# A gated delta-rule layer on one core: setup memsets split over three engines, the last batch's z moved into its scan, and the gating and storing of complete batches moved forward

## The chip, the cores and the metric

The kernel runs on one core of one Trainium2 chip. The metric is the device time of one execution in microseconds (us); lower is better. The other seven cores are idle. All arithmetic is fp32.

The engines are named as the profile names them: PE is TensorE (matmuls; PEld are its weight loads), DVE is VectorE, ACT is ScalarE, POOL is GpSimd, SP is SyncE, which issues most DMAs here. Each runs its own list of instructions in order, and they meet at semaphores only.

## The reference, cut to what matters

For four batches of 512 tokens of width 256:

```python
xn = layernorm(x)
s  = attn(xn)                    # below
g  = silu(ffn(xn))               # router, 8 experts, a shared expert
out = x + s * g

# attn: 32 value heads on 16 key heads, 128 wide
mixed = silu(causal_conv4(xn @ W_qkv));  q, k, v = split(mixed)
z = xn @ W_z
beta = sigmoid(xn @ W_b);  decay = -exp(A_log) * softplus(xn @ W_a + dt_bias)
for t in range(T):               # per batch and head, S is 128x128
    S = S * exp(decay[t])
    S = S + beta[t] * outer(k[t], v[t] - k[t] @ S)
    o[t] = q[t] @ S
s = (rmsnorm(o) * norm_w * silu(z)) @ W_out
```

## The kernel before, in words

Three blocks of code run one after the other. `prepare_block` normalises x and makes the decays. `ffn_block` computes `gate` = silu(ffn), 16 tiles of 128 tokens by 256, kept in SBUF. It ends at about 433 us. `recurrent_block` is the rest and the place of the change.

`recurrent_block` walks 16 key heads (i) by 4 batches (b), 64 steps, all unrolled. A step works on one batch and the two value heads of one key head, in four chunks of 128 tokens. It is a software pipeline over three batches: while step (i, b) projects and convolves q, k, v of batch b, it also scans the batch before it (b-1), and gates, transposes and projects out the one before that (b-2). The output of each head is summed into `acc` (128 x 16 tiles x 256) by `add_out` (L1209), one half batch at a time. The order on every engine is written out by hand; `counts(i, b)` (L598) turns a step into semaphore values, which all start from BASE.

*The setup* (L1030 to L1052, L1227 to L1245, L1437 to L1443, L787 to L790). Each engine raises its own semaphores, 7 on POOL, 14 on ACT, 16 on DVE and 21 on PE. DVE then clears eleven tiles, PSUM bank TRI and small rows; POOL clears z and acc; ACT clears nothing. All four wait until `init` is 5. SP meanwhile loads the first weights, cols and `sums_row` (1 MB, L609). Then POOL runs `log_decays` (L1420), which needs `sums_row`; ACT scales the output weights, and runs `exp_decay` (L1016) on POOL's result before its first `first_tap` (L1044).

*The scan* is four helpers on each engine. For chunk c, PE: `read_state` (L675, two products with the 128x256 state; the second into the OUT bank), `solve` (L685, the inverse times the residual, into the SCAN bank), `attend` (L700, the state's update at L706 and the scores' product at L713). ACT: `take_state_part` (L966), `take_updates` (L960, the copy `upd`), `squares` (L974). DVE: `residual` (L1161), `new_state` (L1170), `output` (L1183). One chunk's chain is read, residual, solve, upd, update, new state, and round again.

*After step 63* the last scan (batch 3 of the last head) has no step to hide in. PE runs `join_w` to `gated_transpose`, then all four pieces of `project_z` for batch 3, two to a PSUM bank (Z_BANK, banks 5 and 3), waiting for ACT's `gate_z` (L995) between the halves and once more before the output projection, whose OUT_BANK is bank 3 as well. Then four chunks of scan with one piece of `project_out` (batch 2) in each. Then POOL's `output_norms` (L1406), DVE's `gating` (L1197), PE's transposes (L948) and `project_out` for batch 3, and the two `add_out` halves. Then DVE multiplies all four batches of `acc` by `gate` (L1396), adds x to all four (L1401, from `x_back`, tiles whose work is over, loaded by SP from L662), raising `final` for each, and SP, which waits for `final` to be 4, stores four batches of 512 KB (L664 to L667) and waits for them.

Of the kernel before, what the change touches and what calls it, by code (L numbers as in the profile page):

```python
# [14 lines left out]
ALU = mybir.AluOpType  # L15
# [457 lines left out]
def recurrent_block(nc, x, w_in_dram, w_z_dram, w_out_dram, norm_dram, keep, g_rows, out):  # L473
# [10 lines left out]
    with ExitStack() as ctx:  # L484
# [72 lines left out]
        GT_BANK, OUT_BANK, Z_BANK = (0, 2), (3, 1), (5, 3)  # L557
# [29 lines left out]
        x_in, stored, final = sem("x_in"), sem("stored"), sem("final")  # L587

        XT = NL + 1
        X8 = 2 * R - 2  # L590
# [12 lines left out]
        def _(sp):  # L603
# [60 lines left out]
            sp.wait_ge(final, BATCH)  # L664
            for b in range(BATCH):
                sp.dma_start(out[b].rearrange("(c p) d -> p c d", p=P), acc[:, b * NC_:(b + 1) * NC_, :]).then_inc(stored, 16)
            sp.wait_ge(stored, 16 * BATCH)  # L667
# [3 lines left out]
        def _(pe):  # L671
# [68 lines left out]
            def project_z(tb, c):  # L740
                for m in range(KT):
                    last = nc.tensor.matmul(ps[Z_BANK[c // 2]][:, (c % 2) * D:(c % 2 + 1) * D],  # L742
                                            xnT[:, m, tb * T + c * C:tb * T + (c + 1) * C], w_z[:, m, :],
                                            start=(m == 0), stop=(m == KT - 1))
                if c % 2:
                    last.then_inc(z_ps, 1)
# [43 lines left out]
            pe.wait_ge(init, 5)  # L790
# [140 lines left out]
            for c in range(NC_):  # L931
                project_z(BATCH - 1, c)
                if c == 1:
                    pe.wait_ge(z_done, n(2) + 1)
            for c in range(NC_):
                if c:
                    read_state(c)
                solve(c)
                if c == 0:
                    pe.wait_ge(z_done, n(2) + 2)  # L940
                project_out(n, c, NK + 1)
                attend(c)
# [12 lines left out]
        def _(act):  # L955
# [39 lines left out]
            def gate_z(n, h):  # L995
# [3 lines left out]
                nc.scalar.activation(z[:, 2 * h:2 * h + 2, :], ps[Z_BANK[h]][:, :].rearrange("p (c d) -> p c d", c=2),  # L999
# [30 lines left out]
            for s in (decay_done, conv0_done, mixed_done, ksq_done, qsq_done, v_done, wq_done, w32_done, w64_done,  # L1030
                      z_done, fs_done, upd_done, osq_done, gT_done):
                act.sem_inc(s, BASE)
            act.wait_ge(norm_in, 16)
            act.wait_ge(init, 5)
# [106 lines left out]
            gate_z(n, 0)  # L1141
            gate_z(n, 1)
            for c in range(NC_):
                if c:
                    take_state_part(c)
                take_updates(c)
                squares(c)
# [5 lines left out]
        def _(dve):  # L1153
# [77 lines left out]
            for t in (qkT[1], v[1], kw[1], scores[1], inv[0], inv[1], invT, bmat, xq, xqT, o):  # L1231
# [13 lines left out]
            dve.wait_ge(init, 5)  # L1245
# [132 lines left out]
            halves(n, 1)  # L1378
            for c in range(NC_):
# [4 lines left out]
                output(c)  # L1384
            add_out(n, BATCH - 2, 0)
            add_out(n, BATCH - 2, 1)
            n = counts(NK, 1)
            for g in range(REP):
                gating(n, g)
            add_out(n, BATCH - 1, 0)  # L1390
            add_out(n, BATCH - 1, 1)

            dve.wait_ge(acc_done, n(2) + 2)
            for b in range(BATCH):
                at = slice(b * NC_, (b + 1) * NC_)
                nc.vector.tensor_tensor(acc[:, at, :], acc[:, at, :], gate[:, at, :], ALU.mult).then_inc(acc_done, 1)  # L1396
            dve.wait_ge(x_in, 16 * BATCH)
            dve.wait_ge(acc_done, n(2) + 2 + BATCH)
            for b in range(BATCH):
                row = acc[:, b * NC_:(b + 1) * NC_, :].rearrange("p c d -> p (c d)")  # L1400
                nc.vector.tensor_tensor(row, row, x_back[b], ALU.add).then_inc(final, 1)  # L1401
# [3 lines left out]
        def _(pool):  # L1405
# [33 lines left out]
            for t in (z, acc):  # L1439
                nc.gpsimd.memset(t[:, :, :], 0.0).then_inc(init, 1)  # L1440
            pool.sem_inc(init, 1)
            pool.wait_ge(init, 5)
# [167 lines left out]
```

## Time and profile before

| | |
|---|---|
| runs (us) | 2793.66, 2805.60, 2795.55; median 2795.55 |
| profiled execution, its own time | 2802.01 |
| its span, first to last instruction | 2800.1 |
| mean granted TensorE clock | 0.985 of 2.4 GHz |
| busy: PE, DVE, ACT, POOL | 94%, 71%, 58%, 38% |
| prepare and FFN blocks end, recurrence's setup begins | about 433 |
| first matmul of step 0 | 445.88 |
| first matmul after step 63 (the last `join_w`) | 2736.29 |
| last output of the scan done | 2767.93 |
| first store issued | 2792.07 |

How to read it: rows of a timeline give the start in us from the span's beginning, the length, the engine and line, output <- input, and how many instructions were merged; in square brackets how long the engine had idled before it and who released it. A length of merged rows is from the first's start to the last's end. A PE group's busy end is modelled, so the start of the next group tells more than the length. SPq is SP's queue issuing a DMA. PEclk is the granted clock: 1.00 is 2.4 GHz, 0.50 is 1.2 GHz.

### The profile page before, as it was taken

The page shows a single profiled execution, that of the slowest core. Times are in us where ns is not written, and L with a number is a line of the kernel's source. Part 1 is how long each engine was busy: PE and PEld are TensorE (multiplying, and loading weights), DVE is VectorE, ACT ScalarE, POOL GpSimd, SP SyncE. Part 2 cuts the span into 40 slices and gives each one's busy share as a digit, 9 for nine tenths or more (in the row PEclk, how much of TensorE's full clock was granted, in tenths as well). Part 3 has the DMA queues.
Part 4 walks back from the last instruction along what each step waited for, and adds up shares of the span by engine and source line. Part 5 has one row for each costly group of instructions (what it writes and reads, how often), then busy time and mean ns, then how long its engine had stood idle before and what let it go on. Part 6 is the DMA issues. An engine that isn't in the chain of part 4 may idle for free.

```text
span 2800.1 us, 87430 instructions
## 1 busy us (share of the span) xinstructions
PE 2619.4 (94%) x34330; PEld 1946.0 (69%) x34330; DVE 2001.6 (71%) x4880; ACT 1610.8 (58%) x5046; POOL 1075.5 (38%) x1391
## 2 busy tenths in 40 slices
PE   2999997999999999999999999999999999999995
PEld 2456655777777777777777777777777777777774
DVE  5322235888878887888778877887778878888773
ACT  2111114666666666666666666666666666666662
POOL 0312203444444444444444444444444444444440
PEclk8999998999999999999999999999999999999997
DMA  4322301111111111111111111111111111111112
GB/s 148 76 53 64 64 1 53 46 54 46 53 46 54 46 54 46 54 46 54 46 53 46 54 46 53 47 43 49 43 49 50 49 49 50 50 50 50 50 50 64
DMA packets 225654, 146.99 MB, mean 52 GB/s; under 512 B 187456, under 2 KB 195936, under 8 KB 225120
## 3 DMA queue, kind: packets, MB, share of 16 engines
q1 hardware_dynamic: 219104, 123.58, 15.5%
q0 software_dynamic: 6144, 17.83, 2.8%
q8 instruction: 275, 4.51, 0.7%
q14 instruction: 131, 1.07, 0.1%
HBM read 115.81 MB, written 2.70 MB: 42 GB/s over the span
## 4 chain that ended last, share of the span: by engine, by line
PE 66%; DVE 8%; ACT 3%; issue 2%; DMA 2%; SPq 1%; POOL 1%; DVEq 0%; POOLq 0%; ACTq 0%
PE rps L809 12%; PE rps L734 8%; PE rps L742 8%; DVE conv L1262 6%; PE rps L696 4%; PE rps L826 4%; PE rps L713 4%; PE rps L865 3%; PE rps L856 3%; PE rps L839 3%; PE rps L680 3%; PE rps L706 3%; PE rps L774 3%; PE rps L783 3%; PE rps L683 2%
## 5 line engine op out<-in xcount | busy, mean ns | idle before, releaser
L1262 DVE SCALAR_TENSOR_TENSOR conv<-rps,w_in,conv 128x509 f32<-128x509 f32 (+2 forms) x768 | 572.0, 745 | 64.6 <-ACT conv L1050 46.4
L809 PE MATMUL rps<-xnT,w_in 128*128 128x512 f32 x1024 | 504.3, 615 | 13.9 <-DVE cols L1244 13.0
L1461 POOL TENSOR_TENSOR decay_b<-decay,beta_k 128x512 f32<-128x512 f32 x128 | 130.6, 1042 | 487.6 <-DVE beta_k L1278 487.6
L1412 POOL TENSOR_TENSOR o_t<-o_sq,q_mean 128x8 f32<-128x8 f32 x65 | 13.4, 206 | 691.0 <-ACT gated L983 691.0
L809 PEld LDWEIGHTS rps<-xnT,w_in 128*128 128x128 f32 x1024 | 174.8, 190 | 148.2 <-issue 125.2
L742 PE MATMUL rps<-w_z,xnT 128*128 128x256 f32 x1040 | 275.1, 387 | 1.0 <-ACT z L999 0.7
L1050 ACT ACTIVATE conv<-rps,w_in 128x512 f32<-128x512 f32 x256 | 176.1, 688 | 164.5 <-PE rps L809 161.5
L734 PE MATMUL rps<-w_outn,gatedT 128*128 128x256 f32 x1056 | 241.3, 381 | 1.0 <-ACT gatedT L993 0.7
L734 PEld LDWEIGHTS rps<-w_outn,gatedT 128*128 128x128 f32 x1056 | 201.6, 191 | 49.7 <-issue 23.8
L1064 ACT ACTIVATE qkT<-conv 128x512 f32<-128x512 f32 x128 | 80.5, 629 | 222.1 <-DVE conv L1262 222.1
L742 PEld LDWEIGHTS rps<-w_z,xnT 128*128 128x128 f32 x1040 | 183.1, 191 | 21.6 <-ACT z L999 1.1
L964 ACT ACTIVATE upd<-rps 128x256 f32<-128x256 f32 x260 | 100.0, 385 | 158.9 <-PE rps L696 158.3
L983 ACT ACTIVATE gated<-o 128x128 f32<-128x128 f32 x520 | 155.1, 304 | 59.7 <-DVE o L1188 57.4
L435 DVE TENSOR_TENSOR silu_g<-fps_u,silu_g 128x512 f32<-128x512 f32 x51 | 35.3, 692 | 196.6 <-PE fps_u L458 196.6
L1022 ACT ACTIVATE decay<-log_d,cols 128x128 f32<-128x128 f32 x520 | 165.9, 395 | 5.0 <-POOL log_d L1435 4.3
L1435 POOL TENSOR_TENSOR log_d<-log_d,sums_row 128x512 f32<-128x512 f32 x130 | 163.3, 1277 | 5.4
L398 POOL DMA_DIRECT2D scale<-comb_rows x96 | 64.2, 679 | 247.6 <-DVE hid L424 187.2
L713 PE MATMUL rps<-upd,scores 128*128 128x128 f32 x1040 | 158.4, 275 | 0.0
L1337 DVE TENSOR_TENSOR xq<-rps,xq 128x256 f32<-128x256 f32 x128 | 53.9, 421 | 142.1 <-PE rps L865 142.1
L1206 DVE SCALAR_TENSOR_TENSOR gated<-o,o_r,z 128x128 f32<-128x128 f32 x528 | 151.4, 344 | 2.2 <-POOL o_r L1418 2.1
L1167 DVE SCALAR_TENSOR_TENSOR resid<-rps,cols,v 128x128 f32<-128x128 f32 x390 | 118.3, 345 | 43.9 <-PE rps L680 43.7
L409 ACT ACTIVATE silu_g<-fps_g 128x512 f32<-128x512 f32 x68 | 40.6, 597 | 189.0 <-PE fps_g L458 189.0
(217 smaller groups left out, 6477.4 us busy)
## 6 DMA issues: line engine op xcount, KB each, us to landing
sums_row<-g_rows SPq DMA_DIRECT2D x65, 1024.0 KB, 5.0
scale<-comb_rows POOLq DMA_DIRECT2D x40, 256.0 KB, 5.0
w_in<-in_w_in SPq DMA_DIRECT2D x17, 520.0 KB, 3.5
bq<-bmat SPq DMA_DIRECT2D x256, 32.0 KB, 2.0
inv<-xq SPq DMA_DIRECT2D x256, 32.0 KB, 1.9
w_z<-in_w_z SPq DMA_DIRECT2D x17, 256.0 KB, 2.6
w_out<-in_w_out SPq DMA_DIRECT2D x17, 256.0 KB, 5.0
invT<-xqT SPq DMA_DIRECT2D x128, 32.0 KB, 2.2
```

Of the source, the lines that this page charges most:

```text
L713: last = nc.tensor.matmul(ps[OUT][:, g * P:(g + 1) * P], scores[r][:, g * NC_ + c, :], upd[:, g * P:(g + 1) * P], start=True, stop=True)
L734: last = nc.tensor.matmul(ps[OUT_BANK[c // 2]][:, (c % 2) * D:(c % 2 + 1) * D], gatedT[:, g, c * C:(c + 1) * C], w_outn[:, g, :], start=(g ...
L742: last = nc.tensor.matmul(ps[Z_BANK[c // 2]][:, (c % 2) * D:(c % 2 + 1) * D], xnT[:, m, tb * T + c * C:tb * T + (c + 1) * C], w_z[:, m, :] ...
L809: last = nc.tensor.matmul(ps[PROJ_BANK[j]][:, :], w_in[:, m * 4 * P + j * P:m * 4 * P + (j + 1) * P], xnT[:, m, b * T:(b + 1) * T], start= ...
L983: last = nc.scalar.activation(gated[:, c, g * P:(g + 1) * P], o[:, c, g * P:(g + 1) * P], ACT.Square, accum_out=o_sq[:, u:u + 1])
L1022: last = nc.scalar.activation(decay[:, u, :], log_d[:, u, :], ACT.Exp, bias=col(k, NLO, u))
L1050: nc.scalar.activation(conv[:, j, :], ps[PROJ_BANK[j]][:, :], ACT.Copy, scale=w_in[:, KT * 4 * P + j * KC + KC - 1:KT * 4 * P + (j + 1) * ...
L1167: nc.vector.scalar_tensor_tensor(resid[:, g * P:(g + 1) * P], ps[SCAN][:, g * P:(g + 1) * P], col(k, NGAM, u), v[r][:, u, :], ALU.mult, AL ...
L1206: nc.vector.scalar_tensor_tensor(gated[:, c, part], o[:, c, part], o_r[:, u:u + 1], z[:, c, part], ALU.mult, ALU.mult).then_inc(gated_done, 1)
L1262: nc.vector.scalar_tensor_tensor(conv[:, j, shift:T], ps[PROJ_BANK[j]][:, 0:T - shift], w_in[:, k:k + 1], conv[:, j, shift:T], ALU.mult, A ...
L1435: nc.gpsimd.tensor_tensor(log_d[:, us, :], log_d[:, us, :], sums_row[:, 1, us, :], ALU.add).then_inc(g_done, 1)
L1461: nc.gpsimd.tensor_tensor(decay_b[:, us, :], decay[:, us, :], beta_k2[:, us].unsqueeze(2).to_broadcast([P, NC_, C]), ALU.mult).then_inc(db ...
```

## The change

Four edits, all in `recurrent_block`.

1. Setup: DVE keeps qkT, v, kw, bmat, xq, xqT and the small ones; POOL clears inv[0], inv[1], invT and z; ACT clears scores[1], o and acc, by a copy of a constant column with scale 0. `init` counts 9.
2. z of batch 3: the block of four `project_z` calls ahead of the last scan goes. Each chunk now has one between `solve` and `project_out`. The second half goes to bank 4 instead of 3, and PE's two waits for `z_done` go. ACT's two `gate_z` calls move from before the scan to behind `take_updates` of chunks 1 and 3.
3. Gate and x: batch 0's product with `gate` stands behind `output(0)` of the last scan, batch 1's behind `output(1)`, batch 0's x behind `output(2)`, batch 1's x behind the two `add_out` of batch 2. Batch 2 has both behind the last `gating`. Batch 3 is done in halves of 128x512, each as add, product, x.
4. Stores: SP stores batches 0 to 2 each as `final` reaches 1, 2, 3, and batch 3 in two halves of 256 KB at 4 and 5.

```diff
-        GT_BANK, OUT_BANK, Z_BANK = (0, 2), (3, 1), (5, 3)
+        GT_BANK, OUT_BANK, Z_BANK, LAST_Z = (0, 2), (3, 1), (5, 3), (5, 4)
...
+        INIT = 9
...
-            sp.wait_ge(final, BATCH)
-            for b in range(BATCH):
+            for b in range(BATCH - 1):
+                sp.wait_ge(final, b + 1)
                 sp.dma_start(out[b].rearrange("(c p) d -> p c d", p=P), acc[:, b * NC_:(b + 1) * NC_, :]).then_inc(stored, 16)
-            sp.wait_ge(stored, 16 * BATCH)
+            for h in range(2):
+                sp.wait_ge(final, BATCH + h)
+                sp.dma_start(out[BATCH - 1].rearrange("(c p) d -> p c d", p=P)[:, 2 * h:2 * h + 2, :],
+                             acc[:, TILES - NC_ + 2 * h:TILES - NC_ + 2 * h + 2, :]).then_inc(stored, 16)
+            sp.wait_ge(stored, 16 * (BATCH + 1))
...
@@ tensor, after step 63
             for c in range(NC_):
-                project_z(BATCH - 1, c)
-                if c == 1:
-                    pe.wait_ge(z_done, n(2) + 1)
-            for c in range(NC_):
                 if c:
                     read_state(c)
                 solve(c)
-                if c == 0:
-                    pe.wait_ge(z_done, n(2) + 2)
+                project_z(BATCH - 1, c, LAST_Z)
                 project_out(n, c, NK + 1)
                 attend(c)
...
@@ scalar, setup
+            for t in (scores[1], o, acc):
+                flat = t[:, :, :].rearrange("p a n -> p (a n)")
+                nc.scalar.activation(flat, cst[:, IDENT:IDENT + 1].to_broadcast(list(flat.shape)), ACT.Copy, scale=0.0).then_inc(init, 1)
@@ scalar, after step 63
-            gate_z(n, 0)
-            gate_z(n, 1)
             for c in range(NC_):
                 if c:
                     take_state_part(c)
                 take_updates(c)
+                if c % 2:
+                    gate_z(n, c // 2, LAST_Z)
                 squares(c)
...
@@ vector, setup
-            for t in (qkT[1], v[1], kw[1], scores[1], inv[0], inv[1], invT, bmat, xq, xqT, o):
+            for t in (qkT[1], v[1], kw[1], bmat, xq, xqT):
                 nc.vector.memset(t[:, :, :], 0.0)
@@ vector, after step 63
+            def times_gate(tiles, done):
+                at = slice(*tiles)
+                dve.wait_ge(acc_done, done)
+                nc.vector.tensor_tensor(acc[:, at, :], acc[:, at, :], gate[:, at, :], ALU.mult).then_inc(mul_done, 1)
+
+            def plus_x(tiles, muls):
+                b, t0 = tiles[0] // NC_, tiles[0] % NC_
+                dve.wait_ge(x_in, 16 * BATCH)
+                dve.wait_ge(mul_done, muls)
+                row = acc[:, slice(*tiles), :].rearrange("p c d -> p (c d)")
+                nc.vector.tensor_tensor(row, row, x_back[b][:, t0 * D:(t0 + tiles[1] - tiles[0]) * D], ALU.add).then_inc(final, 1)
...
             for c in range(NC_):
                 if c:
                     residual(c)
                 if c < NC_ - 1:
                     new_state(c)
                 output(c)
+                if c < 2:
+                    times_gate(whole[c], n(2))
+                if c == 2:
+                    plus_x(whole[0], 1)
             add_out(n, BATCH - 2, 0)
             add_out(n, BATCH - 2, 1)
+            plus_x(whole[1], 2)
             n = counts(NK, 1)
             for g in range(REP):
                 gating(n, g)
-            add_out(n, BATCH - 1, 0)
-            add_out(n, BATCH - 1, 1)
-
-            dve.wait_ge(acc_done, n(2) + 2)
-            for b in range(BATCH):
-                at = slice(b * NC_, (b + 1) * NC_)
-                nc.vector.tensor_tensor(acc[:, at, :], acc[:, at, :], gate[:, at, :], ALU.mult).then_inc(acc_done, 1)
-            dve.wait_ge(x_in, 16 * BATCH)
-            dve.wait_ge(acc_done, n(2) + 2 + BATCH)
-            for b in range(BATCH):
-                row = acc[:, b * NC_:(b + 1) * NC_, :].rearrange("p c d -> p (c d)")
-                nc.vector.tensor_tensor(row, row, x_back[b], ALU.add).then_inc(final, 1)
+            times_gate(whole[BATCH - 2], n(2))
+            plus_x(whole[BATCH - 2], 3)
+            for h in range(2):
+                add_out(n, BATCH - 1, h)
+                times_gate(part[h], n(2) + h + 1)
+                plus_x(part[h], 4 + h)
...
@@ gpsimd, setup
-            for t in (z, acc):
+            for t in (inv[0], inv[1], invT, z):
                 nc.gpsimd.memset(t[:, :, :], 0.0).then_inc(init, 1)
-            pool.sem_inc(init, 1)
-            pool.wait_ge(init, 5)
+            pool.wait_ge(init, INIT)
```

`whole` lists the tiles of each batch, `part` the two halves of batch 3. The waits of PE, ACT and DVE for `init` change from 5 to `INIT` too.

## Rows read from the trace of the kernel before

**Rows 1.** The page's busy times of the engines (busy us, share of the span, instructions).
```profile
PE 2619.4 (94%) x34330; PEld 1946.0 (69%) x34330; DVE 2001.6 (71%) x4880; ACT 1610.8 (58%) x5046; POOL 1075.5 (38%) x1391
```
**Rows 2.** Timeline of the setup: start us, length us, engine line op, [idle before <-releaser].
```profile
435.04 3.51 POOL L1440 MEMSET acc<- 128x4096 f32 x1
435.36 0.91 DVE L1232 MEMSET qkT<- 128x1024 f32 x1 [32.19 <-issue]
...
435.98 0.59 SPq L609 DMA_DIRECT2D sums_row<-g_rows  x1
436.44 0.91 DVE L1232 MEMSET v<- 128x1024 f32 x1 [0.16 <-issue]
...
445.91 1.89 POOL L1426 TENSOR_TENSOR log_d<-sums_row,cols 128x1024 f32<-128x1024 f32 x1 [7.36 <-DVE cols L1244]
```
**Rows 3.** The view of line 609, the first sums_row load: issue to landing.
```profile
DMA to landing us min/median/max: 6.9/6.9/6.9
```
**Rows 4.** Timeline, ACT's decay exponentials of step 0.
```profile
451.86 2.45 ACT L1022 ACTIVATE decay<-log_d,cols 128x128 f32<-128x128 f32 x8 [3.93 <-POOL log_d L1435]
```
**Rows 5.** Timeline, PE from the z block to the first projection of the last scan.
```profile
2747.14 3.09 PE L742 MATMUL rps<-w_z,xnT 128*128 128x256 f32 x8
...
2752.81 0.61 PE L696 MATMUL rps<-v,inv 128*128 128x128 f32 x4
...
2753.72 1.13 PE L734 MATMUL rps<-w_outn,gatedT 128*128 128x256 f32 x4 [0.30 <-ACT z L999]
```
**Rows 6.** Timeline, the last scan's chunk 1 and the beginning of chunk 2.
```profile
2755.78 0.42 DVE L1193 COPY o<-rps 128x256 f32<-128x256 f32 x1
2755.81 0.70 PE L680 MATMUL rps<-state,qkT 128*128 128x256 f32 x2
...
2756.55 0.61 DVE L1167 SCALAR_TENSOR_TENSOR resid<-rps,cols,v 128x128 f32<-128x128 f32 x2 [0.34 <-PE rps L680]
...
2757.76 1.03 PE L734 MATMUL rps<-w_outn,gatedT 128*128 128x256 f32 x4
...
2758.62 0.61 PE L706 MATMUL rps<-upd,kw 128*128 128x128 f32 x4
...
2759.93 0.70 PE L680 MATMUL rps<-state,qkT 128*128 128x256 f32 x2 [0.25 <-DVE state L1177]
2760.67 0.61 DVE L1167 SCALAR_TENSOR_TENSOR resid<-rps,cols,v 128x128 f32<-128x128 f32 x2 [0.46 <-PE rps L680]
```
**Rows 7.** Timeline from the last scan's end to the stores.
```profile
2767.86 1.28 DVE L1212 TENSOR_TENSOR acc<-rps,acc 128x512 f32<-128x512 f32 x2
...
2769.31 1.64 POOL L1416 TENSOR_TENSOR o_n<-o_t,mhalf 128x8 f32<-128x8 f32 x1
...
2771.26 2.19 DVE L1206 SCALAR_TENSOR_TENSOR gated<-o,o_r,z 128x128 f32<-128x128 f32 x8 [2.13 <-POOL o_r L1418]
...
2780.10 0.69 DVE L1212 TENSOR_TENSOR acc<-rps,acc 128x512 f32<-128x512 f32 x1 [6.65 <-PE rps L734]
...
2782.67 4.63 DVE L1396 TENSOR_TENSOR acc<-acc,gate 128x1024 f32<-128x1024 f32 x4
...
2792.07 3.40 SPq L666 DMA_DIRECT2D out<-acc  x4
```
**Rows 8.** ACT's groups by shape: busy us, mean ns, idle before.
```profile
L964 ACT ACTIVATE upd<-rps 128x256 f32<-128x256 f32 x260 | 100.0, 385 | 158.9 <-PE rps L696 158.3
...
L993 ACT ACTIVATE gatedT<-rps 128x512 f32<-128x512 f32 x132 | 78.4, 594 | 22.7 <-PE rps L725 16.3 <-PE rps L948 6.4
```
**Rows 9.** Line 1206 from 445 to 451: duration in ns, min/median/max.
```profile
L1206 DVE SCALAR_TENSOR_TENSOR gated<-o,o_r,z x4: 342/1328/2089, 445.9 to 449.3; 128x128 f32<-128x128 f32 x4
```
**Rows 10.** Windows: busy us of PE, PEld, DVE, ACT, POOL; granted clock, DMA share, GB/s.
```profile
456.20:490.40 34.20, 33.26 (x438) 25.82 (x433) 26.02 (x66) 22.86 (x75) 13.99 (x16) 0.96 0.08 21
...
2749.50:2767.90 18.40, 15.56 (x84) 12.09 (x82) 4.94 (x16) 6.58 (x24) 0.00 (x0) 1.00 0.00 1
```
**Rows 11.** The view of line 666, the four stores: issue to landing.
```profile
DMA to landing us min/median/max: 3.0/4.6/5.5
```

More of the change, by code:

```diff
@@ L586, in recurrent_block @@
         b8_done, b8_ps, x8_done = sem("b8_done"), sem("b8_ps"), sem("x8_done")
-        x_in, stored, final = sem("x_in"), sem("stored"), sem("final")
+        x_in, stored, mul_done, final = sem("x_in"), sem("stored"), sem("mul_done"), sem("final")
         XT = NL + 1
+        INIT = 9
         X8 = 2 * R - 2
@@ L738, in project_out, with project_z @@
                     last.then_inc(out_ps, 1)
-            def project_z(tb, c):
+            def project_z(tb, c, banks=Z_BANK):
                 for m in range(KT):
-                    last = nc.tensor.matmul(ps[Z_BANK[c // 2]][:, (c % 2) * D:(c % 2 + 1) * D],
+                    last = nc.tensor.matmul(ps[banks[c // 2]][:, (c % 2) * D:(c % 2 + 1) * D],
                                             xnT[:, m, tb * T + c * C:tb * T + (c + 1) * C], w_z[:, m, :],
@@ L789, in _ @@
                 pe.sem_inc(s, BASE)
-            pe.wait_ge(init, 5)
+            pe.wait_ge(init, INIT)
             for i in range(NK):
@@ L993, in take_transposes, with gate_z @@
                 nc.scalar.activation(gatedT[:, g, :], ps[GT_BANK[g]][:, :], ACT.Copy).then_inc(gT_done, 1)
-            def gate_z(n, h):
+            def gate_z(n, h, banks=Z_BANK):
                 act.wait_ge(gated_done, n(8) + 8)
                 act.wait_ge(z_ps, n(2) + h + 1)
-                nc.scalar.activation(z[:, 2 * h:2 * h + 2, :], ps[Z_BANK[h]][:, :].rearrange("p (c d) -> p c d", c=2),
+                nc.scalar.activation(z[:, 2 * h:2 * h + 2, :], ps[banks[h]][:, :].rearrange("p (c d) -> p c d", c=2),
                                      ACT.Silu).then_inc(z_done, 1)
@@ L1032, in _ @@
                 act.sem_inc(s, BASE)
+            for t in (scores[1], o, acc):
+                flat = t[:, :, :].rearrange("p a n -> p (a n)")
+                nc.scalar.activation(flat, cst[:, IDENT:IDENT + 1].to_broadcast(list(flat.shape)), ACT.Copy, scale=0.0).then_inc(init, 1)
             act.wait_ge(norm_in, 16)
[L1034 removed]
+            act.wait_ge(init, INIT)
             scale_out_weights(1)
@@ L1244, in _ @@
             nc.vector.memset(cols[BATCH - 1][:, :], 0.0).then_inc(init, 1)
-            dve.wait_ge(init, 5)
+            dve.wait_ge(init, INIT)
             for i in range(NK):
@@ L1378, in _ @@
             halves(n, 1)
+            def times_gate(tiles, done):
[8 more added lines that the diff above has]
+                nc.vector.tensor_tensor(row, row, x_back[b][:, t0 * D:(t0 + tiles[1] - tiles[0]) * D], ALU.add).then_inc(final, 1)
+            whole = [(b * NC_, (b + 1) * NC_) for b in range(BATCH)]
+            part = [(TILES - NC_, TILES - 2), (TILES - 2, TILES)]
             for c in range(NC_):
```

## The prediction

> **What bounds the kernel now.** The page's busy shares come first: TensorE is busy 94% of the span [rows 1], nearly all of it in the 64 equal steps of the recurrence, which the diff does not touch. So only two stretches can change: the setup before step 0, and what follows step 63. I read the timeline of each, because a mean over the span hides both.
>
> Setup: DVE clears its tiles one after the other, a 1024-column tile each 1.08 us, from 435.36 on, while POOL is through with its largest one at 438.55. PE, ACT and POOL all start behind DVE's last memset, POOL's log decays at 445.91 [rows 2]. The sums_row load that these decays read was issued at 435.98 [rows 2] and took 6.9 us [rows 3], so it landed at 442.88. The first decay exponentials on ACT wait for POOL until 451.86 [rows 4], and ACT's first convolution copy stands behind them in its queue. So POOL's start places step 0.
>
> End: from 2747.14 PE does nothing but the last batch's z, before the scan's first solve at 2752.81 [rows 5]. Then come four scan chunks of 4.12 us each (read of the state at 2755.81, the next at 2759.93) [rows 6]; norms, gating, transposes and output projection until the first add at 2780.10; gate and x passes over all batches on DVE; and the stores, issued from 2792.07 [rows 7].
>
> **The change part by part.**
>
> *Memsets.* DVE loses four 1024-column tiles (scores, both inv, o) and the half-size invT. At 1.08 us a tile [rows 2] and about 0.6 for the half, 4.9 us: DVE would be done near 441.0, 4.9 before 445.9. POOL trades acc (4096 columns, 3.51 us [rows 2]) for 2560 more columns elsewhere and ends earlier than now. ACT gets 6144 columns in three activations. Its copies take 0.385 us for 256 columns and 0.594 for 512 [rows 8], 0.21 per 256 more: 1.0, 1.0 and 3.5 us. Starting near DVE's first memset, it ends near 441 too. Bounds for ACT: 5.5 us by that slope, 7.1 as twelve times the 512-column row; I take the slope, since one long instruction pays its start once, and even 7.1 ends at 442.5. That is below the next limit, sums_row at 442.88. POOL then starts near 442.95 instead of 445.91: **3.0 us**, where the memsets alone would give 4.9. PE's first projection starts earlier still, but its later work waits for ACT, behind POOL's decays.
>
> *The z block.* PE no longer runs z from 2747.14 to 2752.81 (5.67 us), nor waits 0.30 for ACT's z [rows 5]. Added are four pieces of z, one a chunk, between solve and projection. A piece has as many instructions of 256 columns as a projection piece, which takes 0.86 from its start to the next group's [rows 6] at the full clock; at the lower level it is half of 3.09, some 1.5 [rows 5]. What could hide it is the wait from solve to ACT's upd, but the projection fills that already: the group behind it starts 0.86 after it with no wait shown [rows 6]. So z costs its full price: 0.86 in each of chunks 1 to 3, and in chunk 0, partly at 1.2 GHz, 1.4, with 0.45 more because the first solve moves into that slow stretch. Chunk 1 begins 5.67 + 0.30 - 1.4 - 0.45 = 4.1 earlier; the three others give 2.6 back. ACT's two z activations (0.6 each [rows 8]) run while PE is in z and projection, and the next user, squares, waits for a later o: no cost.
>
> *Gate and x inside the scan.* A whole-batch pass takes 1.16 us, four in 4.63 [rows 7]. Three lie on DVE in chunks 0 to 2 (two gates, one x), between output(c) and residual(c+1). In the first gap DVE idles 0.34, in the second 0.46 [rows 6], so a pass delays the residual by 0.8, 0.7 and 0.7, and PE's solve stands right behind it: 2.2 lost. Bounds: 0 if DVE overlapped all of it, 3.5 if all three counted whole. The x pass of batch 1 stands behind the two add_outs, which end at 2769.14, and is done by 2770.3, before the gating's 2771.26 [rows 7]: hidden, 0.9 to spare. Both passes of batch 2 lie behind the gating, while PE transposes and projects until 2780.10: hidden, with several us of idle DVE left.
> Beside that x pass POOL works on the norms, 1.64 us of it in one instruction [rows 7]. Next to POOL's setup work DVE's gating, an instruction with two SBUF inputs, took up to 2.09 us where it otherwise takes 0.34 [rows 9]; the x pass has two SBUF inputs as well. The Trainium skill (GPSIMD Engine Reference, Key points) says that GpSimd shares its SBUF interfaces with VectorE and contends with such instructions. The row and this rule speak against that one place; POOL's operands there are 128x8 against 128x1024 in the setup, so the sum has no hold in it, and the hold is a rival.
> Scan in all: -4.1 + 2.6 + 2.2 = **0.7 us later**, if the clock stays full as now [rows 10].
>
> *The last batch.* From the first add (2780.10) to the first store issue (2792.07) are 11.97 us [rows 7]. New are six instructions of 512 columns (add, gate, x, twice). An add takes 0.69 [rows 7]; with about 0.05 for each wait on its own result, 4.4 us: **7.6 us** less. PE's second half is ready within the first three, so DVE sets this stretch.
>
> *Stores.* Now 8.0 us from the first issue to the end of the span. The fastest of the four 512 KB stores landed 3.0 us after its issue, the slowest 5.5 [rows 11]. Three now leave under other work, and the last one moves 256 KB. Bounds 2 and 3.5 us; I take 2.5 (the fastest, less what half the bytes save), and 0.5 to the last instruction: **5.0 us** less. SP waits in order, but each earlier final comes long before the next.
>
> Sum: 3.0 - 0.7 + 7.6 + 5.0 = **14.9 us**. The profiled execution took 2802.01 (span 2800.1), so it would take 2787.1. It lies 6.5 above the median of the runs, 2795.55, so the forecast is 2795.55 - 14.9 = **2780.6**. A measurement of this kernel can tell about 0.5%, 14 us, from no change: the sum is just beyond it.
>
> **The rivals.**
> *The memsets decide alone.* If sums_row landed earlier, the setup would give 4.9: 2778.7. Against it: the load's time hangs on the loads around it, and none of them moves.
> *A held DVE.* If POOL's 1.64 us norm holds the x pass as in [rows 9], the pass ends as late as 2772.2 and pushes the gating by up to 0.9: 2781.5. If the three passes in the scan also cost their whole 3.5 us, 2782.8. For: the same two engines did it in the setup. Against: the small operands.
> *The lower clock.* PE waits longer in each chunk. A chunk has about 3 us of PE work in its chain (z and projection 0.86 each; read, solve and update some 0.45 each, by groups of 0.6 to 0.7 that overlap [rows 6]). At 1.2 GHz that adds 3 us in three chunks and 2 in chunk 0: 11 us, 2791.6. Against: the scan idles already (15.56 us of work in 18.4) and is granted 1.00 [rows 10], and z adds work.
> *No earlier stores.* If the first three stores still left together with the last, 4 us of the five would be lost: 2784.6. The ascending counts on final speak against it.
> *Slower than before.* Step 0 begins after other gaps than now. It has 33.26 us of PE work in 34.2 at a mean clock of 0.96 [rows 10]. If PE, idle before its second projection, stayed at 1.2 GHz through the whole step, about 30 us would come on: 2810. Against: in the run shown it left that level early in the step. It decides against the change once half of the step is slow.
>
> **How the numbers follow.** Forecast 0.62, its own range 2777 to 2784; the terms' bounds and the spread of a median split it into 0.42 beyond 0.5% and 0.20 within. Memsets alone 0.08 (faster). Held DVE 0.16 (0.03 faster, 0.13 within). Lower clock 0.07 and late stores 0.05 (within). Slower 0.02. Together: faster 0.53, same 0.45, slower 0.02. The range goes from 2775 (memsets alone, a 2 us store, and a fast median) to 2788 (held passes, late stores and a slow median); the lower clock and the slower case stay out.
>
> **What would show it.** POOL's log decays 2.9 us earlier, behind the load and not behind a memset. Chunks of 5.6 to 5.8 us instead of 4.12, the residual late behind a DVE pass; the last output of the scan within 1 us of its old place. From the first add of the last batch to the last store issue 4.4 us, from there to the end 3. The forecast is wrong if PE's clock is 0.50 in the scan, if z costs a chunk nothing (2.6 us more won), if the load lands at another time, or if one of the 64 steps changes its length.

## The result, and the profile after

| us | before | after |
|---|---|---|
| median (lowest to highest) of nine runs each, on the same chip | 2800.76 (2793.66 to 2805.60) | 2787.56 (2786.54 to 2795.24) |
| profiled execution, own time (span) | 2802.01 (2800.1) | 2787.04 (2785.2) |

The ratio after to before is 0.9956, with a 95% interval from 0.9947 to 0.9965: 12.3 us faster, between 9.8 and 14.8, which is just inside the 0.5% that was called the bound. The two profiled executions differ by 14.9 us, the medians by 13.2.

The page after shows the same shares as before [rows 1], so it says nothing of where the time went:

```profile
PE 2622.0 (94%) x34330; PEld 1947.0 (70%) x34330; DVE 1994.5 (72%) x4877; ACT 1614.6 (58%) x5049; POOL 1073.6 (39%) x1393
```

The stages do. Each boundary of this table is the start of one row in the timelines; the times are differences between such starts, in us.

| stage | before | after | gain |
|---|---|---|---|
| FFN's last ACT instruction to POOL's first log decays | 12.97 | 10.00 | 2.97 |
| from there to the last `join_w` (64 steps) | 2290.38 | 2288.93 | 1.45 |
| last `join_w` to the last output's combination on DVE | 31.22 | 32.06 | -0.84 |
| from there to DVE's gating (norms) | 3.75 | 4.60 | -0.85 |
| gating to the last batch's first add | 8.84 | 8.69 | 0.15 |
| first add to the end of DVE's work | 11.94 | 4.33 | 7.61 |
| from there to the end of the span | 8.06 | 3.26 | 4.80 |

That is 15.3 us; the FFN ended 0.39 later, which leaves the 14.9. The diff has nothing in the 64 steps, so the 1.45 there isn't its doing: over the fourteen profiles of this study that stage lies between 2286.4 and 2297.6 us. That spread is as large as the one between the runs of one kernel, and probably the reason for it, though the profiles, which are of different kernels and chips, can't show that. The other stages repeat more closely: from the last `join_w` to the end, a second profile of this kernel and one with another order of loads took 52.5 and 53.5 us against 52.94 here.

**Setup.** The timeline of the kernel after, from the memsets to step 0's log decays:

```profile
434.95 1.06 ACT L1035 ACTIVATE scores<-cst 128x1024 f32<-128x1024 f32 x1 [1.24 <-PEq L372]
435.75 0.91 DVE L1235 MEMSET qkT<- 128x1024 f32 x1 [32.20 <-issue]
436.37 0.59 SPq L610 DMA_DIRECT2D sums_row<-g_rows  x1
436.86 3.60 ACT L1035 ACTIVATE acc<-cst 128x4096 f32<-128x4096 f32 x1
...
441.41 1.14 DVE L1209 SCALAR_TENSOR_TENSOR gated<-o,o_r,z 128x128 f32<-128x128 f32 x4
...
443.33 1.89 POOL L1443 TENSOR_TENSOR log_d<-sums_row,cols 128x1024 f32<-128x1024 f32 x1 [5.60 <-DMA sums_row<-g_rows]
```

POOL's release is now the load and not a DVE memset [rows 2]. ACT's two visible clears took 1.06 and 3.60 us, close to the 1.0 and 3.5 of the prediction.

**The scan.** The timeline after, PE and DVE from the first solve to chunk 2's read, and chunk 3's read (the reads are the rows of L685):

```profile
2743.09 1.18 PE L701 MATMUL rps<-v,inv 128*128 128x128 f32 x4
2744.06 1.91 PE L747 MATMUL rps<-w_z,xnT 128*128 128x256 f32 x4
2745.77 1.43 PE L739 MATMUL rps<-w_outn,gatedT 128*128 128x256 f32 x4
...
2748.16 0.70 PE L685 MATMUL rps<-state,qkT 128*128 128x256 f32 x2
2748.47 1.22 DVE L1386 TENSOR_TENSOR acc<-acc,gate 128x1024 f32<-128x1024 f32 x1
...
2749.60 0.60 DVE L1170 SCALAR_TENSOR_TENSOR resid<-rps,cols,v 128x128 f32<-128x128 f32 x2
...
2750.26 0.71 PE L701 MATMUL rps<-resid,inv 128*128 128x128 f32 x4 [0.95 <-DVE resid L1170]
...
2750.80 1.03 PE L747 MATMUL rps<-w_z,xnT 128*128 128x256 f32 x4
...
2751.67 1.03 PE L739 MATMUL rps<-w_outn,gatedT 128*128 128x256 f32 x4
...
2753.84 0.70 PE L685 MATMUL rps<-state,qkT 128*128 128x256 f32 x2 [0.25 <-DVE state L1180]
...
2759.41 0.70 PE L685 MATMUL rps<-state,qkT 128*128 128x256 f32 x2 [0.25 <-DVE state L1180]
```

Chunks take 5.68 and 5.57 us instead of 4.12 [rows 6]. z stands from 2750.80 to 2751.67, 0.87 us that the chunk is longer by, and PE waits 0.95 us for a residual that stands behind the gate pass. The windows (columns as in [rows 10]) show the clock:

```profile
2743.10:2746.80 3.70, 3.70 (x12) 3.17 (x12) 0.00 (x0) 0.98 (x2) 0.00 (x0) 0.53 0.56 177
2746.80:2764.30 17.50, 14.24 (x78) 11.35 (x76) 7.69 (x17) 6.30 (x23) 0.00 (x0) 1.00 0.09 31
```

For 3.7 us of chunk 0 it is mostly at 1.2 GHz, then at 2.4 to the end of the scan.

**The end.** The timeline after, from the last output to the last pieces:

```profile
2764.32 0.42 DVE L1191 TENSOR_TENSOR o<-rps,from_state 128x256 f32<-128x256 f32 x1 [2.98 <-PE rps L718]
...
2765.86 1.25 DVE L1393 TENSOR_TENSOR acc<-acc,conv 128x1024 f32<-128x1024 f32 x1
2766.11 2.49 POOL L1433 TENSOR_TENSOR o_n<-o_t,mhalf 128x8 f32<-128x8 f32 x1
...
2768.92 2.19 DVE L1209 SCALAR_TENSOR_TENSOR gated<-o,o_r,z 128x128 f32<-128x128 f32 x8 [1.81 <-POOL o_r L1435]
...
2777.61 0.69 DVE L1215 TENSOR_TENSOR acc<-rps,acc 128x512 f32<-128x512 f32 x1 [4.03 <-PE rps L739]
2778.33 0.69 DVE L1386 TENSOR_TENSOR acc<-acc,gate 128x512 f32<-128x512 f32 x1
...
2779.85 2.50 SPq L670 DMA_DIRECT2D out<-acc  x2
...
2781.25 0.69 DVE L1393 TENSOR_TENSOR acc<-acc,log_d 128x512 f32<-128x512 f32 x1
```

One row is new in kind: POOL's norm on 128x8 elements takes 2.49 us, beside DVE's x pass, where it took 1.64 [rows 7]. The view of line 1433 over the whole span says how rare that is: the two lowest figures are a minimum and a median of 65, the last is this one.

```profile
L1433 POOL TENSOR_TENSOR o_n<-o_t,mhalf x65: 1635/1637/2492, 486.1 to 2766.1; 128x8 f32<-128x8 f32 x65
```

### The profile page after: what moved, and what is told of

It reads as the page before. It is cut to its first block, busy times and chain, and to the rows that moved or that the text cites. A ratio compares the mean times of both kernels' runs of the same rounds, so it can differ in the third digit from the quotient of the medians.

```text
span 2785.2 us, 87436 instructions
## 1 busy us (share of the span) xinstructions
PE 2622.0 (94%) x34330; PEld 1947.0 (70%) x34330; DVE 1994.5 (72%) x4877; ACT 1614.6 (58%) x5049; POOL 1073.6 (39%) x1393
## 3 DMA queue, kind: packets, MB, share of 16 engines
q1 hardware_dynamic: 219120, 123.58, 15.3%
## 4 chain that ended last, share of the span: by engine, by line
PE 66%; DVE 8%; ACT 3%; issue 2%; DMA 2%; SPq 1%; POOL 1%; DVEq 0%; POOLq 0%; ACTq 0%
PE rps L814 12%; PE rps L739 8%; PE rps L747 8%; DVE conv L1265 6%; PE rps L701 4%; PE rps L831 4%; PE rps L718 4%; PE rps L870 3%; PE rps L861 3%; PE rps L844 3%; PE rps L685 3%; PE rps L711 3%; PE rps L779 3%; PE rps L788 3%; PE rps L688 2%
## 5 line engine op out<-in xcount | busy, mean ns | idle before, releaser
L1429 POOL TENSOR_TENSOR o_t<-o_sq,q_mean 128x8 f32<-128x8 f32 x65 | 13.2, 204 | 691.1 <-ACT gated L983 691.1
```

## The experiments

Ratios are against the kernel before, run beside the others on one chip. Stages are those of the table above, from one profiled execution of each kernel; the "before" and "after" of a stage are those of that table, which may come from another chip.

**Each part alone.** `setup` is the kernel before with only the memsets divided.

```diff
-            for t in (z, acc):
+            for t in (inv[0], inv[1], invT, z):
...
+            for t in (scores[1], o, acc):
...
-            for t in (qkT[1], v[1], kw[1], scores[1], inv[0], inv[1], invT, bmat, xq, xqT, o):
+            for t in (qkT[1], v[1], kw[1], bmat, xq, xqT):
```

> Before with the split of the memsets alone. Theory (sums_row's landing is the next limit): POOL's log decays start 3.0 us earlier than in the kernel before, released by the load, and the time falls by 3.0 us. Rival (the memsets alone decide): 4.9 us earlier, 4.9 us less. Rival (the gain is lost again in step 0 by a lower granted clock): the first steps end as late as before, 0 us.

Measured: 0.9990 (0.9980 to 1.0000), medians 2804.62 against 2807.26. The setup stage took 9.23 us, 3.74 less than before. The forecast had 3.0; the other 0.7 is there because the load landed 6.1 us after its issue and not 6.9. The 3.0 us expected of the whole run (a ratio of 0.9989) fit the interval, and so does no gain at all; the stage shows it. POOL is released by the load:

```profile
442.46 1.89 POOL L1429 TENSOR_TENSOR log_d<-sums_row,cols 128x1024 f32<-128x1024 f32 x1 [4.82 <-DMA sums_row<-g_rows]
```

`setup_rows` adds to it that SP issues the cols and sums_row loads ahead of norm_w and w_in.

```diff
+            sp.dma_start(cols[0][:, :], prep[:, 0:1, :]).then_inc(cols_in, 16)
+            sp.dma_start(sums_row[:, :, :, :].rearrange("p k u t -> p k (u t)"), ...).then_inc(rows_in, 16)
             sp.dma_start(norm_w[:, :], norm_dram).then_inc(norm_in, 16)
             sp.dma_start(w_in[:, :], w_in_dram[0]).then_inc(win_in, 16)
```

> The same, and cols and sums_row are issued as SP's first loads instead of its last. If sums_row's landing is what holds POOL, its decays start right behind the last memset, 4.5 to 4.9 us earlier than before, and the time is 1.5 to 1.9 us under that of the split alone. If the landing does not matter, both are equal. w_in then lands later (by about the 5 us of the big load) and PE's first projection could wait for it, which costs nothing as long as it ends before ACT's decay exponentials.

Measured: 0.9976 (0.9967 to 0.9986), medians 2801.71 against 2807.26. The setup stage took 8.13 us, 4.84 less than before. Against `setup` that is 1.10 less and not the 1.5 to 1.9 expected, because the load of `setup` had itself landed early. The timeline; here the load lands 5.0 us after its issue at 434.74:

```profile
441.59 4.85 DVE L1209 SCALAR_TENSOR_TENSOR gated<-o,o_r,z 128x128 f32<-128x128 f32 x4
441.64 1.89 POOL L1429 TENSOR_TENSOR log_d<-sums_row,cols 128x1024 f32<-128x1024 f32 x1 [3.73 <-DVE cols L1247]
...
442.62 3.72 PE L809 MATMUL rps<-xnT,w_in 128*128 128x512 f32 x4 [9.14 <-DMA w_in<-in_w_in]
```

With the load out of the way DVE's last memset releases POOL again, and the gain is the 4.9 that the prediction gave to the memsets alone. So the load was the limit. The w_in load now holds PE instead, and DVE's gating falls into POOL's work, as it did in the kernel before [rows 9], and takes 4.85 us for four instead of the 1.14 of the kernel after.

`zonly` is the kernel before with only z moved under the scan.

```diff
             for c in range(NC_):
-                project_z(BATCH - 1, c)
...
                 solve(c)
+                project_z(BATCH - 1, c, LAST_Z)
                 project_out(n, c, NK + 1)
```

> Before with z of the last batch moved into the scan alone. Theory (z costs its full price in each chunk): the scan's chunks take 4.12 + 0.87 = 5.0 us, chunk 1 begins 3.6 to 4.1 us earlier, the scan ends 1.0 to 1.5 us earlier, and the time falls by as much. Rival (z hides under the wait for upd): chunks stay at 4.1 us and the time falls by 3.6 to 4.1.

Measured: 0.9990 (0.9978 to 1.0002), medians 2804.45 against 2807.26. From the last `join_w` to the last output it took 29.68 us, 1.54 less than before, with the first solve 5.85 earlier and chunks of 4.99 and 4.98: each has z's 0.87 in full. Of the 1.54 the last batch's stage gives 0.90 back (12.84 us against 11.94, see "The clock in the last batch" below), so that to the end 0.74 is left of 63.81. The z move alone is worth less than these runs resolve.

`gates` is the kernel after with the memsets and z put back, so it has the gate and x passes and the stores of the change alone.

> Before with the earlier gates, x passes and stores alone (z block and memsets as before). Theory: each of three chunks is 0.6 to 0.8 us longer (2.0 in all), POOL's pow instruction beside the x pass of batch 1 takes 2.5 instead of 1.64 us (0.85), the stretch from the first add of the last batch to the last store issue takes 4.4 instead of 12.0 (7.6 less) and the stores 4.8 less: 9.5 us less in all. Rival (the passes hide in DVE's idle time): 12.4 us less.

Measured: 0.9958 (0.9942 to 0.9974), medians 2795.32 against 2807.26. The part behind the last `join_w` took 53.98 us, 9.83 less than before; chunks took 4.82 and 4.71, 0.70 and 0.59 more than before. That is close to the 9.5 expected, and this part carries the change. It has the long norm too:

```profile
2774.14 1.25 DVE L1395 TENSOR_TENSOR acc<-acc,conv 128x1024 f32<-128x1024 f32 x1
2774.40 2.49 POOL L1435 TENSOR_TENSOR o_n<-o_t,mhalf 128x8 f32<-128x8 f32 x1
```

**The x pass beside POOL's norm.** `x_late` is the kernel after with that one pass behind the gating.

```diff
             add_out(n, BATCH - 2, 1)
-            plus_x(whole[1], 2)
...
+            plus_x(whole[1], 2)
             times_gate(whole[BATCH - 2], n(2))
```

> The changed kernel with the x pass of batch 1 moved from beside POOL's norms to behind the gating, where DVE has some 5 us idle. Theory (a DVE instruction with two SBUF inputs holds POOL's pow): the pow takes 1.64 us instead of 2.49, the gating starts 0.85 earlier after the scan's last output (3.75 us instead of 4.60), the time falls by 0.85. Rival (the pow was late for another reason): it stays at 2.49.

Measured: 0.9954 (0.9939 to 0.9970), median 2786.46. `x_first` has the pass ahead of the two adds instead.

```diff
+            plus_x(whole[1], 2)
             add_out(n, BATCH - 2, 0)
             add_out(n, BATCH - 2, 1)
-            plus_x(whole[1], 2)
```

> The changed kernel with the x pass of batch 1 ahead of the two adds, so that the adds, one input in PSUM and one in SBUF, run beside the pow. If only an instruction with two SBUF inputs holds POOL, the pow takes 1.64 us. If any busy DVE does, it takes about 2.5 as in the changed kernel.

Measured: one execution of 2784.43 us, so there is no ratio, and it is read by its rows. First x_late, then x_first:

```profile
2764.78 1.28 DVE L1215 TENSOR_TENSOR acc<-rps,acc 128x512 f32<-128x512 f32 x2
...
2766.23 1.64 POOL L1433 TENSOR_TENSOR o_n<-o_t,mhalf 128x8 f32<-128x8 f32 x1
```

```profile
2762.59 1.22 DVE L1393 TENSOR_TENSOR acc<-acc,conv 128x1024 f32<-128x1024 f32 x1
2763.47 0.39 POOL L1429 TENSOR_TENSOR o_t<-o_sq,q_mean 128x8 f32<-128x8 f32 x1 [31.32 <-ACT gated L983]
2763.72 1.28 DVE L1215 TENSOR_TENSOR acc<-rps,acc 128x512 f32<-128x512 f32 x2
2764.22 1.64 POOL L1433 TENSOR_TENSOR o_n<-o_t,mhalf 128x8 f32<-128x8 f32 x1
```

In both the norm is back at 1.64 us. In x_first it starts while DVE is in an add of 512 columns that has one input in PSUM and one in SBUF, and isn't held; POOL's instruction ahead of it, which starts beside the x pass, takes 0.39 us, where it otherwise takes 0.20. So what holds POOL is the pass with two SBUF inputs and not just any busy DVE; the adds differ from it in width as well (512 columns against 1024), which wasn't varied by itself. From the last output to the gating x_late took 3.74 us against 4.60 after and 3.75 before. x_first took 3.93, by the 0.39. The 0.85 us is shown in the stage; in the whole run (0.9954 against 0.9956) it is lost in the spread.

**Where the passes could stand.** `ahead` takes all four passes out of the scan: both gate passes between the gating and `halves`, both x passes right behind `halves`.

```diff
             for g in range(REP):
                 gating(n, g)
+            times_gate(whole[0], n(2))
+            times_gate(whole[1], n(2))
             halves(n, 1)
+            plus_x(whole[0], 1)
+            plus_x(whole[1], 2)
```

> The changed kernel with both gates and both x passes of batches 0 and 1 ahead of the last scan, where DVE idles 4.7 us twice. Theory (each pass in a chunk delays its residual): chunks fall from 5.6 to 5.0 us, the pow to 1.64, the time by 2.0 + 0.85 = 2.9 us under the changed kernel. Rival (chunks are long from z alone): chunks stay at 5.6 and only the 0.85 is won. A loss: the x loads land near the place where the x passes now stand, so a late load would show as a wait there.

Measured: 0.9943 (0.9927 to 0.9960), median 2782.13. Chunks took 4.98 and 4.99, and the norm 1.64. From the last `join_w` to the end it took 50.74 us, 2.2 less than the kernel after, where 2.9 were expected. But the x passes met a load that had not landed, and the first copy of the state stood behind them:

```profile
2742.95 2.36 DVE L1388 TENSOR_TENSOR acc<-acc,conv 128x1024 f32<-128x1024 f32 x2 [2.73 <-DMA log_d<-in_x]
...
2745.70 0.70 PE L685 MATMUL rps<-state,qkT 128*128 128x256 f32 x2 [1.15 <-DVE state L1184]
```

`zgap` takes z out of the scan as well, to the place where PE waits for DVE ahead of `halves_w`; the passes stay as in the kernel after.

```diff
             join_x(n)
-            halves_w(n)
             pe.wait_ge(acc_done, n(2))
+            for c in range(NC_):
+                project_z(BATCH - 1, c, LAST_Z)
+            halves_w(n)
...
-                project_z(BATCH - 1, c, LAST_Z)
+                if c == 0:
+                    pe.wait_ge(z_done, n(2) + 2)
                 project_out(n, c, NK + 1)
```

> The changed kernel with the four pieces of z between the last join and the halves, where PE waits 3.2 us for the copies of the inverse, and none in the scan. Theory: the four pieces (3.5 us at the full clock) fill that wait, chunks fall by 0.87 each and chunk 0 by about 1.5: 4.0 us less. PE then does not idle ahead of the halves, so the granted clock may stay at 1.00 through them, which gives 2 to 3.5 us more: 6 to 7.5 in all under the changed kernel. Rival: the wait is too short and z pushes the halves back, so 1 to 2 us at most is won.

Measured: 0.9934 (0.9918 to 0.9951), median 2779.39; from the last `join_w` to the end 48.75 us against 52.94 after. That is 4.2 less, the 4.0 of z alone and not the 6 to 7.5 expected with the clock: the rows show that z ran mostly at 1.2 GHz itself, and the last batch's stage took 0.64 more than in the kernel after. First the kernel after, then zgap, PE's rows before the scan:

```profile
2737.37 1.94 PE L779 MATMUL rps<-invT,bmat 64*64 64x64 f32 x16 [3.23 <-issue]
...
2740.28 1.97 PE L788 MATMUL rps<-inv,wh 64*64 64x64 f32 x16
```

```profile
2732.78 5.09 PE L747 MATMUL rps<-w_z,xnT 128*128 128x256 f32 x16
...
2737.80 1.14 PE L779 MATMUL rps<-invT,bmat 64*64 64x64 f32 x16
...
2739.62 1.14 PE L788 MATMUL rps<-inv,wh 64*64 64x64 f32 x16
```

z takes 5.09 us, most of it in what was a 3.23 us wait. The small matmuls behind it then take 1.14 us a group instead of 1.94 and 1.97. The windows of zgap say why:

```profile
2732.78:2735.90 3.12, 3.12 (x13) 2.56 (x9) 2.94 (x10) 0.00 (x0) 0.00 (x0) 0.55 0.25 42
2735.90:2737.80 1.90, 1.90 (x10) 1.39 (x9) 0.41 (x2) 0.60 (x1) 0.00 (x0) 1.00 0.34 100
2737.80:2741.00 3.20, 3.11 (x40) 2.73 (x40) 0.20 (x1) 1.79 (x3) 0.00 (x0) 1.00 1.09 368
```

The clock stands mostly at 1.2 GHz for z's first 3.1 us and at 2.4 GHz from then on, where the kernel after goes through these matmuls and chunk 0's z at the lower level. So the first solve comes no later than in the kernel after (10.84 us behind the last `join_w` against 10.83), though z's 5.09 us are longer than the wait they fill.

**Combinations, and the change again.** All four, and the kernel before, ran on one chip. `after_again` is the kernel after, unchanged.

> The changed kernel itself, beside the others on one chip. By its stages it is 13.8 us under the kernel before (ratio 0.9951). If the first measurement, 0.9956, was the truer one, 12.3.

`rows_a` is it with the loads in setup_rows's order.

> The changed kernel with sums_row and cols loaded first. POOL's decays start behind the last memset, 1.9 us earlier after the FFN block's end than in the changed kernel, and DVE's first gating, which then meets POOL's decays, is held again (4.9 us for four instead of 1.1) at no cost. 1.9 us less than the changed kernel. Rival (the load's landing does not hold POOL): no difference.

`spread` is it with the first two gate passes ahead of `halves`, as in ahead, and both x passes behind the last gating.

> The changed kernel with the two gates of batches 0 and 1 ahead of the halves and their two x passes behind the gating, z and loads as in the changed kernel. Theory: chunks of 5.0 us instead of 5.6 (z alone in them), the pow at 1.64, the scan's start not later: 1.9 + 0.85 = 2.8 us under the changed kernel. Rival: the gates ahead of the halves push back DVE's copy of the inverse, and the scan starts later by as much.

`best` is spread with z as in zgap and the loads as in setup_rows.

> The changed kernel with four moves: sums_row and cols loaded first; z of the last batch ahead of the halves; the gates of batches 0 and 1 ahead of the halves too; the x passes of batches 0 and 1 behind the gating. By the terms measured so far it should be 1.9 (load) + 4.2 (z) + 1.9 (no pass in a chunk) + 0.85 (POOL not held) = 8.9 us under the changed kernel, with chunks of 4.1 us and the pow at 1.64. If the terms overlap (z ahead of the halves already took some of the waits that the passes filled), 6 to 7. Rival: the stores of batches 0 to 2, now issued within 4 us of each other, are still moving when the last half is stored, and its landing takes over 4 us instead of 2.8.

| kernel | ratio (95%) | median | setup | last `join_w` to end |
|---|---|---|---|---|
| before | | 2801.90 | | |
| after_again | 0.9951 (0.9937 to 0.9966) | 2786.87 | 10.04 | 52.50 |
| rows_a | 0.9945 (0.9932 to 0.9957) | 2786.39 | 8.13 | 53.54 |
| spread | 0.9934 (0.9922 to 0.9946) | 2783.33 | 9.78 | 49.59 |
| best | 0.9916 (0.9901 to 0.9930) | 2779.07 | 8.13 | 46.17 |

The change came out as before: 0.9951, 13.7 us. rows_a has the expected 1.9 us in its setup stage, but its ratio lies only 1.7 us under that of after_again and its median 0.5, well inside the intervals: the whole run neither shows the gain nor speaks against it. In the profiled pair its steps took 2293.14 us against 2286.37, well inside the spread of that stage. Whether the gating that POOL now holds (4.86 us for four, as in setup_rows) costs some of it stays open. POOL's first two log decays start 19.71 us apart in rows_a and 19.17 in the kernel after, so it is about half a microsecond at most there.

spread has chunks of 4.99 us and the norm at 1.64, and its 49.59 us are 2.9 less than in after_again, as expected (2.8).

best beats both kernels: 0.9916 is 23.5 us under before, and 9.8 under after by the two ratios, whose intervals don't meet. By the stages it is 8.2 (1.9 in the setup, 6.3 behind the last `join_w`), where 8.9 were expected; the last batch's stage, 5.09 us instead of 4.34, has the rest. Its chunks are back at 4.12 us. Its rows: z, the reads of the state at both ends of chunk 1, and the first and last stores. Three stores leave before the last batch's output is added, the last two at the end:

```profile
2732.84 5.41 PE L747 MATMUL rps<-w_z,xnT 128*128 128x256 f32 x16
...
2744.59 0.70 PE L685 MATMUL rps<-state,qkT 128*128 128x256 f32 x2
...
2748.71 0.70 PE L685 MATMUL rps<-state,qkT 128*128 128x256 f32 x2 [0.25 <-DVE state L1183]
...
2763.39 3.97 SPq L667 DMA_DIRECT2D out<-acc  x3
...
2771.11 3.26 SPq L670 DMA_DIRECT2D out<-acc  x2
...
2771.75 0.69 DVE L1218 TENSOR_TENSOR acc<-rps,acc 128x512 f32<-128x512 f32 x1 [0.67 <-PE rps L739]
```

**The clock in the last batch.** The last row above is the second add of the last batch. In best DVE waits 0.67 us for PE's second half of the projection; in the kernel after that add follows the work on the first half at 2779.74 without a wait. The first add stands at 2768.87 in best, and the windows around it show at which clock PE makes that half:

```profile
2762.00:2771.10 9.10, 7.98 (x22) 6.44 (x23) 6.93 (x8) 1.19 (x2) 0.00 (x0) 0.50 0.49 173
2771.10:2773.20 2.10, 0.61 (x3) 0.19 (x1) 1.39 (x2) 0.00 (x0) 0.00 (x0) 1.00 0.36 125
```

All fourteen profiles fall in line: in each the granted clock is 0.50 while PE transposes and projects the last batch, and what the stage from the first add on takes goes by how long after that add the clock is back at 1.00.

| kernels | clock back, us after the first add | stage, us |
|---|---|---|
| with the old end: before, setup_rows, setup, zonly | 0.1, 0.9, 1.4, 1.9 | 11.94, 12.34, 12.57, 12.84 |
| with the new end: after, after_again, rows_a, x_late, x_first, ahead | -0.3, -0.4, -0.1, 0.3, 0.3, 0.4 | 4.33 or 4.34 |
| with the new end: gates, spread, zgap, best | 1.3, 1.4, 1.9, 2.2 | 4.64, 4.74, 4.97, 5.09 |

So a part of what is won ahead of the last batch can be lost again in it: 0.90 us in zonly, 0.75 in best. No run here tries what would bring the clock back sooner.

## Why the prediction was right and where it was wrong

Two steps failed. In the mechanism it was the x pass beside POOL's norm, whose hold the sum put at nothing and which cost 0.85 us. In the time it was the base, a median of three runs that lay 5.2 us under that of nine. The measured median, 2787.56 us, lies outside the forecast's own range of 2777 to 2784, and only just inside the one with the rivals, which ends at 2788.

The sum was 14.9 us. The profiled executions agree to the tenth, but a part of that is chance: without the 1.45 of the untouched steps the stages give 13.8, and the ratio gives 12.3. Term by term:

- **Memsets, 3.0.** Measured 2.97, by the mechanism given: sums_row's landing. That landing varied between the profiles with this change, from 6.0 to 7.0 us, so this stage came to 9.16 to 10.14 us under the same order of loads. That the load is the limit, setup_rows shows.
- **The z block, 4.1 earlier and 2.6 back.** From `join_w` to chunk 1's read the stages sum to 15.90 us after and 19.52 before, so chunk 1 began 3.6 earlier. The missing half microsecond is chunk 0: the prediction had its z only partly at 1.2 GHz, and the clock rose some 3.5 us after the solve, so z (1.71 to the next start) and some of the projection were at that level. That is luck of the pair as much as an error: the clock was back 14.3 us after the last `join_w` here and 13.2 in the kernel before. In x_late, after_again and zonly it was back after 13.5, and chunk 1 began 4.3, 4.3 and 4.1 earlier than before, which is the forecast's 4.1. The full price of z in the later chunks is confirmed by zonly.
- **DVE passes, 2.2.** Chunks 1 and 2 took 5.68 and 5.57, of which 0.87 is z; 0.69 and 0.58 are the passes. With the third some 1.9 in all. Both errors nearly cancel: the scan ends 0.84 later, 0.7 was predicted. The clock was full in these chunks, as predicted.
- **The last batch, 7.6, and the stores, 5.0.** 7.61 and 4.80. The 7.61 needs a clock that is back by the first add, as it was in both profiles of this pair; the old stage took up to 12.84 us and the new one up to 5.09 where it came later. A 256 KB store landed 2.1 to 2.9 us after its issue:

```profile
DMA to landing us min/median/max: 2.1/2.5/2.9
```

- **The x pass.** This is the step of the mechanism that failed: "hidden, 0.9 to spare", and "the sum has no hold in it", because POOL's operands are small. It costs 0.85 us, the price that the rival of the held DVE named, but with the parts reversed: DVE's pass takes its usual time (1.25) and POOL's norm is held (2.49 against 1.64), and the gating waits for the norm. x_late and x_first show it. The Trainium skill (GPSIMD Engine Reference, Key points), which the prediction weighed against its row and set aside, says that the engines contend where VectorE's instruction has two SBUF inputs, and the two kernels are in keeping with that condition: 2.49 beside such a pass, 1.64 beside an add with one input in PSUM. That section names no side that loses. The runs show either: POOL here, DVE in [rows 9] and setup_rows.
- **The base.** This is the step that put the time off. The time of 2780.6 lies 7.0 us under the median. Of that 5.2 comes from "the median of the runs, 2795.55": it was the median of three, and over nine runs it is 2800.76. The three spanned 12 us, as much as the whole effect. The profiled run's 2802.01 was nearer to the middle than the median was, and the prediction took its 6.5 us off. The other 1.8 are the sum's 14.9 against 13.2 by the medians.

Being beyond or within 0.5% hung on this margin: the ratio's interval (0.35 to 0.53% faster) reaches both sides, and the second measurement's (0.34 to 0.63%) as well. The chances of 0.42 and 0.20 put too much on the far side for a sum with 0.9 us beyond the bound, of which the hold took 0.85. The rivals of the lower clock in the whole scan, of stores that still leave together and of a slow step 0 did not occur (for the last, the granted clock is 0.91 from 453 to 470 us of the kernel after and 1.00 from there to 488); the memsets alone did decide once the loads were turned round, in setup_rows.

What the change left on the table is its places. It put z and three passes into a chain in which PE and DVE release each other and idle 0.25 to 0.5 us at a time, where they cost 2.6 and 1.9 us. PE has a 3.23 us wait right ahead, and DVE waits ahead of the scan and behind the gating: moved there, the gate passes ahead of the scan and the x passes behind the gating, they cost nothing that the stages up to the last batch's first add show. z in PE's wait comes with a clock that is back early: in zgap and best after 4.9 and 5.9 us from the last `join_w`, in the other twelve profiles after 12.3 or more. What is left of the gain then depends on the clock in the last batch.

## What to carry to other kernels

When work is moved "under" something, ask for the longest single idle stretch of its engine and whether the data are there: gaps of a third of a microsecond in a chain of dependent steps covered next to nothing here, and a wait of 3 us a little earlier covered all. Look at the granted clock of the stages behind the gain as well, since work that comes earlier can meet the lower clock. Then look at what the neighbour engine executes beside every DVE instruction with two SBUF inputs, for a tiny instruction of POOL can be the one that suffers, with the chain behind it. And when the expected gain is 0.5%, take the base from the profiled run and many runs, and show each part by its stage, not by the total.

## What the hardware showed that was not expected

- The hold between DVE and POOL falls on either. POOL's 128x8 norm took 2.49 us instead of 1.64 beside one 128x1024 pass of DVE, and its 128x8 product 0.39 instead of 0.20; DVE's gating of 128x128 took 4.85 us for four instead of 1.14 beside POOL's 128x1024 work. Who started first doesn't settle by itself who loses. POOL was held where DVE's pass had begun 0.25 us earlier (the norm) and 0.88 us earlier (the product). But the first of the four gatings, recorded at 445.86, 0.05 us ahead of POOL's 445.91, took the longest, 2.09 us, while POOL's took its usual 1.89 [rows 2] [rows 9]. The shortest, 0.34, stands between two instructions of POOL. What decides it was not tried.
- The clock can fall when PE is busy without a pause. In zgap PE waits 1.00 us ahead of the last `join_w` and 0.48 us behind it, in a stretch of 32x32 matmuls granted 1.00. From 2732.30, in the joins that follow, the granted clock is 0.50, and z starts at 2732.78 at that level, though PE no longer pauses; 1.00 is back by 2735.90. In best it falls 0.7 us after z has begun. So the 5.09 us of z's sixteen matmuls are more than the 3.5 that four times the 0.87 of a full-clock piece would be. It pays all the same, since here the rise comes before the 64x64 matmuls and not in the scan.
- Step lengths wander without any edit: the 64 steps took 2286.4 to 2297.6 us over fourteen profiles from several chips, all at a mean clock of 0.984 to 0.988 over the run. The three longest are from one chip.
